# A linear-attention block with an MLP: 8x8 diagonal inverses on VectorE and one joint step to 32, in place of doubling on TensorE

## The reference, cut to what matters

```python
A0 = -jnp.where(strict, einsum('id,jd->ij', wk, wk) * L, 0.0)   # 64 x 64, strictly lower
A = jnp.linalg.inv(eye - A0)                                   # the inverse of this case
v_new = A @ v - (A @ wk) @ S
o = rk_g @ S + intra @ v_new
S = gamma_C * S + wk_g @ v_new                                 # the state, chunk after chunk
# MLP on the tokens of the chunk
h = silu(lin(x, w1)) * lin(x, w2); h = gelu(lin(h, h1)); h = gelu(lin(h, h2)); y = lin(h, w3)
```

## Time and profile before

| | |
|---|---|
| median of 3 runs | 2082.95 us (2079.86 to 2087.43) |
| the profiled execution | 2082.42 us, span 2080.5 us |
| PE busy | 1978.2 us (95%) |
| DVE busy | 1178.7 us (57%) |
| ACT busy | 1005.4 us (48%) |
| POOL busy | 537.1 us (26%) |
| mean granted TensorE clock | 0.978 |

### The profile page before, as it was taken

The page is one execution under the profiler, slowest core; times in us unless marked ns, Lnnn a source line. Parts: engine busy times, 40 slices in busy tenths (PEclk is TensorE's granted clock), DMA queues, the critical chain, the costliest instruction groups (busy, mean ns, idle before and its releaser), DMA issues.

```text
span 2080.5 us, 82836 instructions
## 1 busy us (share of the span) xinstructions
PE 1978.2 (95%) x36778; PEld 1859.4 (89%) x36778; DVE 1178.7 (57%) x2676; ACT 1005.4 (48%) x2393; POOL 537.1 (26%) x558
## 2 busy tenths in 40 slices
PE   4489999999999999999999999999999999999998
PEld 1389999999999999999999999999999999999998
DVE  5656555556555556655556655555655555665543
ACT  2344544454554455554445454445455445555444
POOL 2323222232222222222222322223222222222210
PEclk7589999999999999999999999999999999999999
DMA  5300000000000000000000000000000000000000
GB/s 184 108 13 18 18 18 13 8 18 18 17 18 17 3 18 17 18 17 18 5 15 18 17 18 17 12 8 18 18 17 18 17 3 18 17 18 17 13 3 12
DMA packets 32212, 44.87 MB, mean 22 GB/s; under 512 B 8125, under 2 KB 24521, under 8 KB 31753
## 3 DMA queue, kind: packets, MB, share of 16 engines
q1 hardware_dynamic: 31144, 37.43, 6.4%
q10 hardware_dynamic: 736, 2.13, 0.3%
HBM read 22.63 MB, written 8.39 MB: 15 GB/s over the span
## 4 chain that ended last, share of the span: by engine, by line
PE 81%; DVE 9%; ACT 4%; issue 3%; POOL 0%; DMA 0%; DVEq 0%; ACTq 0%; POOLq 0%
PE mlp L955 60%; PE duo L1067 5%; PE duo L1050 4%; ACT h L747 3%; PE duo L1108 3%; PE solo L1091 2%; PE mlp L1007 2%; DVE xn L893 2%; PE solo L1080 1%; DVE inv L854 1%; DVE xl L900 1%; PE duo L1074 1%; PE duo L1054 1%; DVE lv L847 1%; PE duo L1099 1%
## 5 line engine op out<-in xcount | busy, mean ns | idle before, releaser
L955 PE MATMUL mlp<-act_hi,w_hi 128*128 128x256 f32 x4096 | 1031.2, 292 | 0.3
L955 PE MATMUL mlp<-act_lo,w_hi 128*128 128x256 f32 x4096 | 993.0, 282 | 0.0
L955 PEld LDWEIGHTS mlp<-act_hi,w_hi 128*128 128x128 f32 x4096 | 780.4, 191 | 17.2 <-DVE act_lo L825 0.4
L955 PEld LDWEIGHTS mlp<-act_lo,w_hi 128*128 128x128 f32 x4096 | 782.5, 191 | 0.8
L825 DVE TENSOR_TENSOR act_lo<-full,act_hi 128x256 fp32r<-128x256 f32 x768 | 347.1, 455 | 690.8 <-ACT act_hi L774 683.5
L773 ACT ACTIVATE full<-mlp,scale_sb 128x256 f32<-128x256 f32 x512 | 242.7, 474 | 750.3 <-PE mlp L955 748.6
L677 POOL TENSOR_TENSOR lv<-gram,level_mask 128x256 f32<-128x256 f32 x320 | 268.8, 865 | 104.7 <-ACT gram L718 94.3
L955 PE MATMUL mlp<-xh,w_hi 128*128 128x256 f32 x1024 | 262.3, 296 | 3.3 <-DVE xl L900 2.0
L955 PE MATMUL mlp<-xl,w_hi 128*128 128x256 f32 x1024 | 246.0, 279 | 0.0
L774 ACT ACTIVATE act_hi<-mlp,scale_sb 128x256 fp32r<-128x256 f32 x512 | 239.2, 467 | 0.0
L639 POOL TENSOR_TENSOR rstd<-ve,minus_half 128x2 f32<-128x2 f32 x64 | 52.0, 812 | 706.3 <-DVE ve L793 706.3
(11 more groups left out here) (132 smaller groups left out, 2433.8 us busy)
## 6 DMA issues: line engine op xcount, KB each, us to landing
wst<-in_wts SPq DMA_DIRECT2D x22, 512.0 KB, 4.3
xin<-in_x SPq DMA_DIRECT2D x64, 128.0 KB, 2.7
out_y<-y SPq DMA_DIRECT2D x64, 128.0 KB, 2.5
kg<-r SPq DMA_DIRECT2D x64, 126.0 KB
wmod_sb<-in_wmod ACTq DMA_DIRECT2D x1, 1536.0 KB, 8.3
kg<-last SPq DMA_DIRECT2D x64, 2.0 KB
last<-r SPq DMA_DIRECT2D x64, 2.0 KB, 1.9
con<-in_const SPq DMA_DIRECT2D x1, 434.0 KB, 7.4
```

The lines of the kernel that those rows point to most:

```text
L955: mm = pe.matmul(dst, *general_ops, start=is_first and i == 0, stop=is_last and i == 1)
```

## The change

The inverse is made in another way up to blocks of 32. DVE inverts the 8x8 diagonal blocks by forward substitution: it packs them into `low` (128 rows x 64), starts `sub` as unit matrices, and then for each column j = 1 to 6 spreads row j over the rows of its block (`stream_shuffle`), multiplies by the column of `low` and subtracts. `expand` writes the result into `inv`, block-diagonal, and transposes it. From 8 to 32 there is one joint step on PE. With N the product of inverse and remaining part inside a block of 32 (N to the fourth is zero), it computes (I - N)(inverse) plus N squared times that: items `n` 1 to 3. The last doubling from 32 to 64 (`mi`, `upd`) stays. `pred` moves from behind l3 item 2 to a place behind `gram`, ahead of l1 item 0, and gets its two parts into other PSUM banks. `u` (v minus the prediction) moves into `intra`. `norm2` moves ahead of l3 item 7. The masks are three in place of six.

```diff
-    chain = [(name, k) for k in range(1, LEVELS) for name in ("mi", "upd")]
-    chain += [(name, 0) for name in ("pred", "new", "state", "attn_out")]
-    mixed = [("start", 0), ("y", 0), ("ln2", 0), ("y", 1), ("gram", 0), ("values", 0)]
-    FILL = {item: 2 for item in chain[:8]}
...
+    mixed = [("start", 0), ("y", 0), ("ln2", 0), ("y", 1), ("values", 0), ("gram", 0), ("pred", 0)]
+    between = [("intra", 0), ("fs", 0), ("fs", 1), ("fs", 2), ("fs", 3), ("expand", 0), ("n", 1), ("n", 2), None, ("n", 3), ("keys", 0), ("mi", 0), None,
+               ("upd", 0), None, ("new", 0), None, ("state", 0), None, ("attn_out", 0), None, None, ("norm2", 0)]
+    for k, item in enumerate(layers):
+        mixed += [item] + [x for x in between[k:k + 1] if x]
+    mixed += [("silu", 0)]
...
+    next_norm = {("n", 1): "stats", ("n", 2): "norm", ("n", 3): "length", ("upd", 0): "unit"}
```

On POOL:

```diff
+                    if name == "gram":
                         for e in range(2):
+                            pool.wait_ge(gram_ready[e], now)
+                            ins = masked(0, 0, e)
+                        ins.then_inc(near_ready, 1)
+                        for e in range(2):
+                            ins = masked(1, 1, e)
+                        ins.then_inc(cross_ready, 1)
+                    if name == "n" and k == 1:
+                        pool.wait_ge(low_ready, now)
+                        for e in range(2):
+                            ins = masked(0, 2, e)
+                        ins.then_inc(far_ready, 1)
```

On DVE (the items `near`, `inv_sum`, `upd` and `turn` of before are gone):

```diff
+                    if name == "fs" and k == 0:
+                        dve.wait_ge(near_ready, now)
+                        dve.tensor_reduce(low[:], lv[0][:].rearrange("p e q (a n) -> p (e q) n a", n=SB), AX.X, ALU.add).then_inc(low_ready, 1)
+                        dve.tensor_copy(sub[:, :, 1:SB], con[:, CO_EYE + 1:CO_EYE + SB].unsqueeze(1).to_broadcast([P, 2 * NP, SB - 1]))
...
+                        dve.tensor_tensor(sub[:, :, 0:1], con[:, CO_EYE:CO_EYE + 1].unsqueeze(1).to_broadcast([P, 2 * NP, 1]), low[:, :, 0:1],
+                                          ALU.subtract).then_inc(sub_ready[0], 1)
+                    if name == "fs" and k > 0:
+                        for j in (2 * k - 1, 2 * k):
...
+                            dve.wait_ge(sub_ready[j - 1], now)
+                            dve.stream_shuffle(sub_row[:], sub[:], [i // SB * SB + j for i in range(HB)]).then_inc(row_ready[j], 1)
+                            dve.wait_ge(row_ready[j], now)
+                            dve.tensor_tensor(sub_term[:], sub_row[:], low[:, :, j:j + 1].to_broadcast([P, 2 * NP, SB]), ALU.mult).then_inc(term_ready[j], 1)
+                            dve.wait_ge(term_ready[j], now)
+                            dve.tensor_tensor(sub[:], sub[:], sub_term[:], ALU.subtract).then_inc(sub_ready[j], 1)
+                    if name == "expand":
...
+                    if name == "n" and k == 1:
+                        dve.wait_ge(step_ready, now)
+                        dve.transpose(step_nt[:].rearrange("p k n -> p (k n)"), step_n[:].rearrange("p k n -> p (k n)")).then_inc(step_t_ready, 1)
```

On PE:

```diff
-                        pe.wait_ge(intra_ready, now)
+                        pe.wait_ge(hT_ready, now)
...
+                        if has_mlp:
+                            pe.wait_ge(h2_ready, n)
...
+                    if name == "n":
...
+                            if k == 1:
+                                mm = pe.matmul(out(duo[0][:, 0, :]), inv_t[rows, m, :], lv[1][rows, e, q, HB * i:HB * (i + 1)], start=True, stop=True)
+                            if k == 2:
+                                mm = pe.matmul(out(duo[0][:, 1, :]), step_n[rows, m, :], step_nt[rows, m, :], start=True, stop=True)
+                            if k == 3:
+                                mm = pe.matmul(out(duo[1][:, 1, :]), square_t[rows, m, :], first_two[rows, m, :], start=True, stop=True)
...
+                        if k == 2:
+                            for e, q, c, i in quarters:
+                                rows, m = quarter(c, i), e * NP + q
+                                mm = pe.matmul(of_head(duo[1][rows, 0, 0:2 * NP * HB])[:, m, :], step_nt[rows, m, :], inv[rows, m, :], start=True, stop=True)
```

More of the change, by code:

```diff
@@ L390, in main @@
     lv = [sb(f"lv{i}", [2, NP, C]) for i in range(2)]
-    near = lv[0][:].rearrange("p e q n -> p (e q) n")
+    low = sb("low", [2 * NP, SB])
+    sub = sb("sub", [2 * NP, SB])
+    sub_row = sb("sub_row", [2 * NP, SB])
+    sub_term = sb("sub_term", [2 * NP, SB])
     inv = sb("inv", [2 * NP, HB])
@@ L445, in main @@
     layers = [(name, m) for name in ("l1", "l2", "l3") for m in range(HK)]
-    chain = [(name, k) for k in range(1, LEVELS) for name in ("mi", "upd")]
-    chain += [(name, 0) for name in ("pred", "new", "state", "attn_out")]
-    mixed = [("start", 0), ("y", 0), ("ln2", 0), ("y", 1), ("gram", 0), ("values", 0)]
-    FILL = {item: 2 for item in chain[:8]}
[L451 to L459, removed]
-    put_after(("l1", 1), ("turn", 0))
-    put_after(("upd", 2), ("intra", 0))
-    put_after(("upd", 4), ("keys", 0))
-    for k in range(1, LEVELS - 1):
-        put_after(("upd", k), ("turn", k))
-    next_norm = {("turn", 2): "stats", ("turn", 3): "norm", ("mi", 4): "length", ("upd", 5): "unit"}
+    mixed = [("start", 0), ("y", 0), ("ln2", 0), ("y", 1), ("values", 0), ("gram", 0), ("pred", 0)]
[5 more added lines that the diff above has]
+    next_norm = {("n", 1): "stats", ("n", 2): "norm", ("n", 3): "length", ("upd", 0): "unit"}
     slot_at = {layers[(len(layers) - 4) * i // (SLOTS - EARLY)]: EARLY + i for i in range(SLOTS - EARLY)}
@@ L738, in part @@
                         act.copy(vn[:].rearrange("p q e n -> p (q e n)"), solo[1][:]).then_inc(vn_ready, 1)
-                    if name == "state":
-                        act.wait_ge(inter_full, now)
-                        act.copy(o_state[:].rearrange("p q n -> p (q n)"), solo[0][:]).then_inc(o_state_ready, 1)
                     if name == "ln2":
@@ new lines, in part @@
+                    if name == "mi":
+                        pe.wait_ge(const_in, 16)
+                        pe.wait_ge(far_ready, now)
+                        pe.wait_ge(inv_t_ready[1], now)
+                        for e, q, c, i in quarters:
+                            if i == 1:
+                                mm = pe.matmul(of_head(duo[0][quarter(c, 0), 0, 0:2 * NP * HB])[:, e * NP + q, :], lv[0][quarter(c, 1), e, q, 0:HB],
+                                               inv_t[quarter(c, 1), e * NP + q, :], start=True, stop=True)
+                        mm.then_inc(mi_full, 1)
@@ new lines, in part @@
+                    if name == "upd":
+                        pe.wait_ge(const_in, 16)
+                        pe.wait_ge(mi_ready, now)
+                        for e, q, c, i in quarters:
+                            rows = quarter(c, i)
+                            if i == 0:
+                                mm = pe.matmul(of_head(duo[0][rows, 1, 0:2 * NP * HB])[:, e * NP + q, :], inv[rows, e * NP + q, :],
+                                               mi[rows, e * NP + q, :], start=True, stop=True)
+                        mm.then_inc(upd_full, 1)
```

164 lines of the change are left out of this document (80 added, 84 removed).

## The result

| | before | after |
|---|---|---|
| median | 2083.72 us (2079.86 to 2087.43, 4 runs) | 2246.91 us (2237.82 to 2247.60, 4 runs) |
| span of the profiled execution | 2080.5 us | 2236.0 us |
| mean granted TensorE clock | 0.978 | 0.903 |
| mean of a step (steps 2 to 30) | 61.8 us | 66.9 us |

The ratio is 1.0773 (95% interval 1.0739 to 1.0807). The direction was right; the time is 51 us above the predicted 2196 us and 12 us above the upper end of the range, 2235 us. (The mean of a step is the distance between the first transposes of one step's `start` and the next's.) Experiments ran on other chips, each beside its own runs of the kernel before, so their ratios are what compares; a hundredth of a ratio is 21 us.

What follows compares the result with a forecast made beforehand. PE's streaming was taken as the bound; per step 7.0 us of stall less 3.9 and 0.97 saved gave +65 us, so 2082.4 + 65 + 46 (clock) + 3 (step 0) = 2196 us, range 2125 to 2235 us.

Steps and rivals of the forecast that it cites:

- PE gives up 3.9 us: On PE, per step: eight visits go (7.04 us), three n items cost 3.20, pred saves 0.1; 3.9 us less.
- DVE's stretch ahead of `n` 1, 11.85 us: DVE works without pause from the first full to the transpose of expand, 11.85 us a step, before PE's n 1.
- The 0.83 us of `fs` 0: In DVE's stretch: a reduction at 0.69 us, a small copy and a small subtraction, with overlaps 0.83 us.
- the 0.4 us of meetings with POOL: In DVE's stretch: 0.4 us a step for operations that meet POOL's masks, the last two beside the first links.
- The rule on the shared port: By an exclusive lock, links meeting a mask could lose a whole mask, 2 us more a step; the sum kept 0.4.
- A link at 0.26 us: Each of 18 chained 128x64 DVE operations takes 0.22 us, 0.26 with hand-off; 4.4 us a step less overlaps.
- PE waits 4.5 us in l1 and 2.4 at `n` 1: PE stands still 7.0 us a step: some 4.5 in l1 items behind full, about 2.4 at n 1.
- The clock, 46 us: After n 1 PE streams 3.4 us at the low clock level, losing 1.5 us a step, +46 us in all.
- the prediction's formula: Clock loss after n 1: low-level time x (1 - 0.12 / 0.21), with 3.4 us giving 1.5 us a step.
- Step 0, +3 us: In step 0, without MLP beside it, DVE's own work grows from 5.5 to some 8.2 us: +3 us.
- The 0.97 us of old waits: PE's waits for xn at y and for inv at the first mi, 0.97 us a step, would go.

Runs made afterwards that it cites:

- e4: Changed kernel reordered: pred, intra and fs 0 behind l1 item 7, rest of substitution behind l2 items, n 1 behind l2 item 5; 1962.92 us, ratio 0.9415.
- e5: Changed kernel with the reduction into low reading each row's elements in order, not with a stride of 8; 2229.68 us, ratio 1.0692.
- e6: Changed kernel with POOL's last two masks waiting for the product of n 1, not for low; 2224.01 us, ratio 1.0657.
- e9: Changed kernel with both the in-order reduction and POOL's last two masks waiting for n 1's product; 2197.32 us, ratio 1.0546.
- e1: Changed kernel with up to 41 filler products a step on PE, in its waits of the l1 stretch; 2190.85 us, ratio 1.0512.

## Why the prediction was right in its direction and wrong in its size

- **PE gives up 3.9 us.** Held for the visits: in e4 the three items `n` cost 0.89, 1.43 and 0.88 us by the prediction's way of reckoning, where it had 0.88, 1.44 and 0.88. The step came out 3.9 us shorter and not 3.9 + 0.97, since 0.9 us of short waits for `full` are left in the l1 items, which the old visits had filled.
- **DVE's stretch ahead of `n` 1, 11.85 us.** This is the step that failed, in two of its terms. In the step shown it is 13.0 us, from 1051.29 to the end of the transpose at 1064.33. The 0.83 us of `fs` 0 and the 0.4 us of meetings with POOL make 1.23; measured are 1.91 and, at the `act_lo`, 0.20, together 2.1. Of these, `fs` 0 by itself is 1.36 and the meetings are 0.75. I took the reduction's price from a row of the same number of inputs, 0.69, though that one reads in order and this one with a stride of 8: 1.15. And I priced the meeting as a share of a mask, from one row of 0.85, where the subtraction lost 0.55 us to one of 0.70. e5, e6 and e9 show both, and without the two the kernel takes 2197 us. The links make up most of the rest, 0.3 us.
- **The rule on the shared port.** The subtraction starts 0.03 us behind a mask, lasts 0.73 and falls to 0.17 when the mask is moved. The Trainium skill, page "SBUF — State Buffer", section "Who interferes with whom", calls the port an exclusive lock, and says that an instruction with two inputs in SBUF takes part and a reduction does not. The trace agrees for the subtraction, which waited 0.55 us for a mask of 0.70. For the reduction no run here shows it: POOL never worked beside one. The links do not meet a mask here, because the two masks are over before they begin; I had looked for the meetings there.
- **A link at 0.26 us.** Held, with the shuffle at 225 ns. A third of the substitution, six links, takes 1.56 us (1056.52 to 1058.08) in place of 4.4 / 3 = 1.47; the second shuffle starts 0.34 us behind the operation before it, not 0.26, with the load of its mask between.
- **PE waits 4.5 us in l1 and 2.4 at `n` 1.** Places right, sizes 3.3 and 1.5, plus 0.6 by "issue": part of the idle time turned into slower products, and the list leaves out what a product's reckoned duration covers.
- **The clock, 46 us.** Held in kind and nearly in size: 54 us or a little more by e1. It stays low 5.5 us behind `n` 1 in the step shown, not 3.4. By the prediction's formula that would be 2.4 us a step, 73 in all; e1 gave back less, and whether the fillers hide the difference stays open. The trace had a fall after a gap of 1.84 us; after, the longest wait of PE is 1.8 us at `n` 1 and 2.2 by "issue", and the fall shown comes after one of 1.42. The Trainium skill, page "TensorE: Matmul & The Clock Gate", section "Why this matters for your kernels", names a long unbroken gap as what takes the clock down. The trace here differs: the clock falls in nearly every step though no wait is longer than those, in the step shown behind a stretch in which PE was busy 4.77 of 6.77 us. The measurement decides: that row alone would have given no fall here.
- **Step 0, +3 us.** Wrong in sign: its `start` is 64.4 us ahead of the next step's, 68.1 before, 3.7 us less. I counted DVE's work alone. Before, PE and DVE waited for each other level by level; after, PE has one long wait, 16.7 us, and the three `n` follow.
- **The 0.97 us of old waits** are gone from their places. But the prediction put all of `y`'s wait down to `xn`; 12.1 of the 30.0 us were waits by "issue", and these come back as 19 us at other places. `pred` with its second part takes 1.49 us in the head (1048.04 to 1049.53), less than the 1.6 of its own work; it does not wait for `h2`.

With the measured sizes the sum is 2196 + 1.2 x 31 (the stretch) + 8 (the clock) - 7 (step 0) = 2234 us. That is 13 below the median, and 4 below the profiled execution, from which these sizes are read.

**Open.** The waits by "issue" have no releaser among the semaphores. They come in about every other step, at the same two places, and grow when DVE's part shrinks. The trace's DMA queues give a lead. One wait of the changed kernel, and what the queues carried from 1201.1 to 1202.2 us:

```profile
1203.49 0.37 PE L977 MATMUL mlp<-act_hi,w_hi 128*128 128x256 f32 x1 [2.19 <-issue]
```

```profile
q8 instruction: 1, 0.02, 5.3%
```

This packet, of the queue that the profile calls `instruction`, landed 1.4 us before the wait ended. From 127 to 1950 us all 17 such waits over 0.3 us in the changed kernel end 1.2 to 1.6 us behind a landing on that queue, and so do 13 of 13 before and 27 of 27 in the kernel without links. Most of the 207 landings in that stretch of the changed kernel have no wait behind them, so a landing alone does not make one. That PE waits there for its own instructions is the likely reading; it is not shown by a run that changes them, nor why these waits grow.

## What to carry over

Before work is moved from the engine that is the bound to one with an average of 57%, look at the stretch in which it lands: here the same instructions cost 163 us beside the l1 items and gained 122 beside the l2 items. A price by the number of elements is not enough: the way the input is read, and what POOL reads in the same instant, made 0.17 into 0.73 us and 0.69 into 1.15. And where small visits are taken out of a stretch in which PE waits, reckon with TensorE's clock as a second loss.

## What was not expected of the hardware

- A reduction of 128x512 to 128x64 takes 678 ns when it reads in order and 1148 ns with a stride of 8 elements.
- A subtraction of 128x8 that starts just behind a POOL mask takes 728 ns, and 174 ns alone: the wait is three times the work.
- The clock fell in nearly every step with no wait of PE above 2.2 us, and 27 products a step put into the idle time of the l1 items and 14 ahead of `n` 1 kept it at 1.00 throughout.
- A shuffle of 128x64 is as cheap as a product or a difference of that size (225 ns), with 13 ns for its mask.
- Every wait of PE by "issue" over 0.3 us in three traces, 57 in all, ended 1.2 to 1.6 us behind a landing on the queue `instruction`.
